# First attention: another order of the query blocks, scores issued further ahead, denominators spread later and copied to SBUF

## The reference

```
q, k, v = _proj_heads(layernorm(x), w_q / w_k / w_v, 16)        # b h s d, d = 16
mask    = triu(-1e8, k=1)
scores  = einsum('bhqd,bhkd->bhqk', q, k) / sqrt(16) + mask
attn    = softmax(scores)
out     = einsum('bhqk,bhkd->bhqd', attn, v)  ->  b s 256  ->  @ w_o
x       = x + out
```

## Time and profile before

| what | us |
|---|---|
| median of 3 runs | 1849.44 |
| lowest and highest run | 1846.48, 1849.45 |
| the profiled execution's own time | 1850.58 |
| its span | 1848.7 |
| TensorE busy in the span | 1626.4 (88%) |
| ScalarE busy in the span | 960.8 (52%) |
| exps of this phase (L711), 640 of them, busy | 514.0 |
| idle time of ScalarE ahead of them | 39.1 |
| weighing matmuls of this phase (L776), busy | 298.9 |

### The profile page before, as it was taken

One profiled execution on the slowest core, in us unless ns is written; L12 is line 12 of the kernel. 1 busy time (PEld: TensorE's weight loads), 2 busy tenths in 40 slices (PEclk: granted clock), 3 DMA queues, 4 the chain that ended last, 5 costly groups with the idle time before them and its releaser, 6 DMA issues. The chain is left out here.

```text
span 1848.7 us, 30826 instructions
## 1 busy us (share of the span) xinstructions
PE 1626.4 (88%) x10249; PEld 1107.8 (60%) x10250; DVE 922.6 (50%) x1792; ACT 960.8 (52%) x1528; POOL 455.8 (25%) x498
## 2 busy tenths in 40 slices
PE   7769999999999966999649999999668977998998
PEld 5632222322222316888638888888567976897887
DVE  6524434434433435777563333333275555755885
ACT  5459999999999953444242222222133335343332
POOL 0001111111111211555542222222153003000674
PEclk9969999999999987999869999999978997998999
DMA  8981415405415019221231111111212010000001
GB/s 265 277 249 35 69 26 93 76 21 91 75 25 88 18 26 326 88 88 46 72 111 48 50 50 51 51 48 51 91 46 92 1 58 0 1 1 4 24 23 46
DMA packets 79455, 134.18 MB, mean 73 GB/s; under 512 B 11600, under 2 KB 45904, under 8 KB 76208
## 3 DMA queue, kind: packets, MB, share of 16 engines
q1 hardware_dynamic: 72360, 111.86, 23.4%
q0 software_dynamic: 6992, 20.95, 3.5%
HBM read 74.63 MB, written 58.14 MB: 72 GB/s over the span
## 5 line engine op out<-in xcount | busy, mean ns | idle before, releaser
L711 ACT ACTIVATE probs<-ps_s 128x1024 f32<-128x1024 f32 (+3 forms) x640 | 514.0, 953 | 39.1 <-PE ps_s L759 36.1
L776 PE MATMUL ps_o<-probs,V 128*17 128x512 f32 (+3 forms) x2560 | 298.9, 539 | 0.3
L699 POOL TENSOR_SCALAR_AFFINE_SELECT probs<-probs 128x512 f32<-128x512 f32 x128 | 86.4, 676 | 468.1 <-ACT probs L711 464.2
L724 DVE COPY weighted<-ps_o 128x512 f32<-128x512 f32 x32 | 22.1, 690 | 255.2 <-PE ps_o L776 255.2
L759 PEld LDWEIGHTS ps_s<-Q_even,K_even 50*128 50x128 f32 x640 | 56.7, 189 | 152.2 <-ACT probs L711 129.4
L1393 DVE COPY slot_hT<-ps_hT 128x512 f32<-128x512 f32 x71 | 49.1, 692 | 194.9 <-PE ps_hT L1436 186.4
L759 PE MATMUL ps_s<-Q_even,K_even 50*128 50x512 f32 (+3 forms) x640 | 128.8, 452 | 18.6 <-DMA Q_even<-shift_parts 10.8
L731 DVE RECIPROCAL inv_denominator<-ps_o 128x512 f32<-128x512 f32 x32 | 107.5, 3358 | 74.5 <-PE ps_o L790 74.5
L759 PEld LDWEIGHTS ps_s<-Q_odd,K_odd 50*128 50x128 f32 x640 | 55.2, 183 | 139.6 <-ACT probs L711 125.6
L1446 PE MATMUL ps_slot_y<-we_out,slot_hT 128*128 x568 | 134.6, 380 | 1.8 <-issue 1.0
L1926 POOL TENSOR_TENSOR h_lo<-h,h_hi 128x512 fp32r<-128x512 f32 x64 | 89.5, 1416 | 181.5 <-DVE h L1972 181.5
(11 more groups left out here) (279 smaller groups left out, 3947.5 us busy)
## 6 DMA issues: line engine op xcount, KB each, us to landing
qk_stacks<-qk_hi SPq DMA_DIRECT2D x64, 256.0 KB, 3.9
slot_rows<-slots_in SPq DMA_DIRECT2D x71, 128.5 KB
qk_stacks<-qk_lo SPq DMA_DIRECT2D x32, 256.0 KB, 4.0
Q_odd<-qk_stacks SPq DMA_DIRECT2D x8, 768.0 KB
K_odd<-qk_stacks SPq DMA_DIRECT2D x8, 768.0 KB
Q_even<-qk_stacks SPq DMA_DIRECT2D x6, 768.0 KB
K_even<-qk_stacks SPq DMA_DIRECT2D x6, 768.0 KB
X<-x SPq DMA_DIRECT2D x8, 512.0 KB, 4.2
```

The costliest lines, as they stand in the source:

```text
L699: pool.affine_select(out=block_of, in_=block_of, compare_op=ALU.is_ge, fill=0.0, base=0, pattern=[[0, HG], [1, P]], channel_multiplier=-1) ...
L711: act.activation(probs[:, at % PROB_BUFS, 2 * p:2 * p + 2, off:BT], ps_s[:, s % SCORE_BUFS, :, off:BT], ACT.Exp).then_inc(exp_ok, 1)
L776: last = pe.matmul(ps_o[32 * h:32 * h + DH + 1, q % 2, off:BT], k["V"][:, group, SEQ_TILES * b + t, h, :], probs[:, at % PROB_BUFS, h, off ...
```

## The change

The order of the blocks within a unit becomes 2, 0, 3, 1 (`TURN`). What used to be counted by `q` (the bank of `ps_o`, the output buffer, the semaphore counts) is counted by the turn `s`, and `q` is looked up only for addresses.

The scores are issued pair by pair. Ahead of the weighing of tile `at`, all pairs below `2 * at + 2 + LEAD` are issued, where LEAD goes by the width of tile `at`: 4 pairs (two tiles ahead) where the tile is 512 or 128 wide, and 6 pairs (three tiles ahead) where it is 384 or 256 wide. In the kernel before it was 4 throughout. The spread of a block's denominators comes after the weighing of the third tile behind the block's last one (the fifth for q = 0), where it was the second. VectorE first copies the spread totals from `ps_o` to SBUF, and then takes the reciprocal within SBUF; the bank of `ps_o` is free from the copy on.

```diff
-    TILE_LIST = [(q, t, max(0, (t - TB * q) * P)) for q in range(SLICES) for t in range(TB * (q + 1))]
+    TURN = (2, 0, 3, 1)
+    TILE_LIST = [(s, t, max(0, (t - TB * TURN[s]) * P)) for s in range(SLICES) for t in range(TB * (TURN[s] + 1))]
...
-    LAG = 2
+    LEAD = {0: 4, P: 6, 2 * P: 6, 3 * P: 4}
+    SPREAD_AFTER = [5 if q == 0 else 3 for q in TURN]
...
                         dve.wait_ge(picked_ok, n + 1)
-                        dve.reciprocal(inv[:, :], ps_o[:, q % 2]).then_inc(norm_ok, 1)
-                        dve.wait_ge(norm_ok, 3 * n + 1)
-                        dve.tensor_tensor(result[:, :], sums[:, q % 2], inv[:, :], ALU.mult).then_inc(norm_ok, 1)
+                        dve.tensor_copy(inv[:, :], ps_o[:, s % 2]).then_inc(norm_ok, 1)
+                        dve.wait_ge(norm_ok, 4 * n + 1)
+                        dve.reciprocal(inv[:, :], inv[:, :]).then_inc(norm_ok, 1)
+                        dve.wait_ge(norm_ok, 4 * n + 2)
+                        dve.tensor_tensor(result[:, :], sums[:, s % 2], inv[:, :], ALU.mult).then_inc(norm_ok, 1)
...
                     if t == 0 and n >= 2:
-                        pe.wait_ge(norm_ok, 3 * (n - 2) + 1)
+                        pe.wait_ge(norm_ok, 4 * (n - 2) + 1)
...
-                for at in range(len(STEPS) + LAG + 2):
-                    if at < len(STEPS):
-                        scores(at)
-                    if 0 <= at - LAG < len(STEPS):
-                        weigh(at - LAG)
-                    if at - LAG - 2 >= 0:
-                        u, g = STEPS[at - LAG - 2]
-                        if g in LAST:
-                            spread_denominators(u, LAST.index(g))
+                scored = 0
+                for at in range(len(STEPS) + SPREAD_AFTER[-1]):
+                    if at < len(STEPS):
+                        for s in range(scored, min(2 * at + 2 + LEAD[TILE_LIST[STEPS[at][1]][2]], 2 * len(STEPS))):
+                            scores(s)
+                            scored = s + 1
+                        weigh(at)
+                    for s in range(SLICES):
+                        u, g = divmod(at - SPREAD_AFTER[s], NT)
+                        if u >= 0 and g == LAST[s]:
+                            spread_denominators(u, s)
```

More of the change, by code:

```diff
@@ L616, in phase_attention @@
     SLICES = SEQ // BT
-    TILE_LIST = [(q, t, max(0, (t - TB * q) * P)) for q in range(SLICES) for t in range(TB * (q + 1))]
+    TURN = (2, 0, 3, 1)
+    TILE_LIST = [(s, t, max(0, (t - TB * TURN[s]) * P)) for s in range(SLICES) for t in range(TB * (TURN[s] + 1))]
     NT = len(TILE_LIST)
-    LAST = [max(g for g, (q, _, _) in enumerate(TILE_LIST) if q == s) for s in range(SLICES)]
-    DIAG = [g for g, (q, t, _) in enumerate(TILE_LIST) if t >= TB * q]
+    LAST = [max(g for g, (at, _, _) in enumerate(TILE_LIST) if at == s) for s in range(SLICES)]
+    DIAG = [g for g, (s, t, _) in enumerate(TILE_LIST) if t >= TB * TURN[s]]
     STEPS = [(u, g) for u in range(UNITS) for g in range(NT)]
     SCORE_BUFS, PROB_BUFS = 3, 4
-    LAG = 2
+    LEAD = {0: 4, P: 6, 2 * P: 6, 3 * P: 4}
+    SPREAD_AFTER = [5 if q == 0 else 3 for q in TURN]
     LOADS = STACK_LOADS + 2
@@ L673, in _ @@
                     g, b = group_and_batch(u)
-                    for q in range(SLICES):
-                        sp.wait_ge(result_ok, SLICES * u + q + 1)
+                    for s, q in enumerate(TURN):
+                        sp.wait_ge(result_ok, SLICES * u + s + 1)
                         for n, out in enumerate((out_hi, out_lo)):
@@ L679, in _ @@
                                 sp.dma_start(io["attended"][n, b, row:row + DH, q * BT:(q + 1) * BT],
-                                             out[32 * h:32 * h + DH, q % 2].bitcast(F32)).then_inc(stored[q % 2], 16)
+                                             out[32 * h:32 * h + DH, s % 2].bitcast(F32)).then_inc(stored[s % 2], 16)
                     if u + 2 < UNITS:
@@ L720, in _ @@
                 for u in range(UNITS):
[L721 to L724, removed]
+                    for s in range(SLICES):
+                        n = SLICES * u + s
+                        dve.wait_ge(pv_ok, NT * u + LAST[s] + 1)
+                        dve.tensor_copy(sums[:, s % 2], ps_o[:, s % 2]).then_inc(sums_ok, 1)
@@ L725, in _ @@
                         dve.wait_ge(sums_ok, 3 * n + 1)
-                        dve.tensor_copy(sums_hi[:, :], sums[:, q % 2]).then_inc(sums_ok, 1)
+                        dve.tensor_copy(sums_hi[:, :], sums[:, s % 2]).then_inc(sums_ok, 1)
                         dve.wait_ge(sums_ok, 3 * n + 2)
-                        dve.tensor_tensor(sums_lo[:, :], sums[:, q % 2], sums_hi[:, :].bitcast(F32), ALU.subtract
+                        dve.tensor_tensor(sums_lo[:, :], sums[:, s % 2], sums_hi[:, :].bitcast(F32), ALU.subtract
@@ L738, in _ @@
-                        dve.wait_ge(norm_ok, 3 * n + 3)
-                        dve.tensor_tensor(out_lo[:, q % 2], result[:, :], out_hi[:, q % 2].bitcast(F32), ALU.subtract
+                            dve.wait_ge(stored[s % 2], 16 * ROWS_OUT * (n // 2))
+                        dve.tensor_copy(out_hi[:, s % 2], result[:, :]).then_inc(norm_ok, 1)
+                        dve.wait_ge(norm_ok, 4 * n + 4)
+                        dve.tensor_tensor(out_lo[:, s % 2], result[:, :], out_hi[:, s % 2].bitcast(F32), ALU.subtract
@@ L744, in _, with scores @@
                 pe.wait_ge(zero_ok, 1)
-                def scores(at):
+                def scores(s):
+                    at, p = s // 2, s % 2
                     u, g = STEPS[at]
                     j = u % 2
-                    q, t, off = TILE_LIST[g]
-                    if g == 0:
+                    turn, t, off = TILE_LIST[g]
+                    q = TURN[turn]
+                    if g == 0 and p == 0:
                         pe.wait_ge(loaded[j], 16 * LOADS * (u // 2 + 1))
@@ L753, in scores @@
                             pe.wait_ge(ones_in, 32)
[L754 to L763, removed]
+                    if s >= SCORE_BUFS:
+                        pe.wait_ge(exp_ok, s - SCORE_BUFS + 1)
+                    for h in range(2):
+                        last = pe.matmul(ps_s[:, s % SCORE_BUFS, h, off:BT],
+                                         K[j][HALF * h:HALF * h + USED_ROWS, p, t * P:(t + 1) * P],
+                                         Q[j][HALF * h:HALF * h + USED_ROWS, p, q * BT + off:(q + 1) * BT],
+                                         start=True, stop=True)
+                    last.then_inc(scores_ok, 1)
                 def weigh(at):
                     u, g = STEPS[at]
-                    q, t, off = TILE_LIST[g]
+                    s, t, off = TILE_LIST[g]
                     group, b = group_and_batch(u)
-                    n = SLICES * u + q
+                    n = SLICES * u + s
                     if t == 0 and n >= 2:
-                        pe.wait_ge(norm_ok, 3 * (n - 2) + 1)
+                        pe.wait_ge(norm_ok, 4 * (n - 2) + 1)
                     pe.wait_ge(exp_ok, 2 * at + 2)
@@ L775, in weigh, with spread_denominators @@
                     for h in range(HG):
-                        last = pe.matmul(ps_o[32 * h:32 * h + DH + 1, q % 2, off:BT],
+                        last = pe.matmul(ps_o[32 * h:32 * h + DH + 1, s % 2, off:BT],
                                          k["V"][:, group, SEQ_TILES * b + t, h, :],
                                          probs[:, at % PROB_BUFS, h, off:BT],
-                                         start=(t == 0), stop=(g == LAST[q]))
+                                         start=(t == 0), stop=(g == LAST[s]))
                     last.then_inc(pv_ok, 1)
-                def spread_denominators(u, q):
-                    n = SLICES * u + q
+                def spread_denominators(u, s):
+                    n = SLICES * u + s
                     if n == 0:
@@ L788, in spread_denominators @@
                     rows = pick[:, :, :].rearrange("p h r -> p (h r)")
-                    pe.matmul(ps_o[:, q % 2], rows, sums_hi[:, :], start=True, stop=False)
-                    pe.matmul(ps_o[:, q % 2], rows, sums_lo[:, :], start=False, stop=True).then_inc(picked_ok, 1)
-                for at in range(len(STEPS) + LAG + 2):
+                    pe.matmul(ps_o[:, s % 2], rows, sums_hi[:, :], start=True, stop=False)
+                    pe.matmul(ps_o[:, s % 2], rows, sums_lo[:, :], start=False, stop=True).then_inc(picked_ok, 1)
+                scored = 0
+                for at in range(len(STEPS) + SPREAD_AFTER[-1]):
                     if at < len(STEPS):
-                        scores(at)
-                    if 0 <= at - LAG < len(STEPS):
-                        weigh(at - LAG)
-                    if at - LAG - 2 >= 0:
-                        u, g = STEPS[at - LAG - 2]
-                        if g in LAST:
-                            spread_denominators(u, LAST.index(g))
```

(8 more changed lines are left out.)

4 lines of the change are left out of this document (1 added, 3 removed).

## The result

The changed kernel took 1825.12 us in the median of 4 runs (1815.60 to 1826.54) against 1848.63 us, the median before once a fourth run is added to the three above; the ratio is 0.9864, with a 95% interval of 0.9829 to 0.9898. Measured once more later, on one chip with three variants, it took 1819.28 us against 1844.82, ratio 0.9853 (0.9829 to 0.9877). So the two differences of medians are 23.5 and 25.5 us. Its profiled execution took 1826.54 us, with a span of 1824.7 us.

What follows compares the result with a forecast made beforehand. ScalarE was taken as the bound wherever the order lets TensorE be ahead. Seven units' 25.9 us plus the first's 1.5, less 0.7 for the copy, give 26.7 us off 1850.58: 1823.9, stated as 1823, range 1813 to 1839.

Steps and rivals of the forecast that it cites:

- TensorE's 60.6 us: TensorE's work in one unit of the first attention, summed from step times: 2.5 us less than ScalarE's.
- a loop that no order takes out: At each block change: exp frees bank, scores, signals, exp tail, 0.75 us against two short exps' 0.56; 0.19 us gap stays.
- restarts: ScalarE starting late after a gap: about 0.1 us each, four in a unit; fewer late ones gain about 0.4 us.
- The price of 1.8 us: Gain a unit from issuing the next block's first scores before the 384-wide weighing: 0.46 us at each of four block changes.
- the spreads' 1.4: Gain a unit from moving the denominator spreads later: 0.75 + 0.46 + 0.2 us of ScalarE's gaps.
- the unit laid out against ScalarE's floor: One attention unit: ScalarE's 63.1 us floor, plus four 0.19 us gaps, four 0.1 us gaps and four 0.1 us restarts, 64.7 us.
- TensorE's stand of 2.4 us: Without the copy, TensorE would wait 2.4 us at q = 3's first weighing for its bank.
- 15.4 us at 2.99 us a tile: First unit's half-clock start: 5.1 full tiles losing 1.16 us each, 6 us, less 1 us for first pairs ahead: 5.
- +0.7 us for the copy: In the phase's last block the added VectorE copy lies on the path, costing 0.7 us once.
- first rival: The three score buffers bound TensorE anyway, so the lead does nothing; only the spreads' gain is left: 1840 us, chance 0.10.
- The masks are not held up: Rival said the SBUF reciprocal delays GpSimd's mask at q = 1's first diagonal tile: 16 us over eight units, 1839, chance 0.05.
- The slower case: Rival: at block changes the later 384-wide weighing holds the exp of the tile four on; 1868 us, chance 0.05.

## Why the prediction was right, and where only by luck

The forecast was 1823 us, 26.7 us less than before in the profiled execution; measured were 24.0 us there, and 23.5 and 25.5 us in the two medians. The unit was forecast rightly; that the total fits is partly luck. The phase itself got 29.3 us shorter in that profile: 4.1 us of gain in the first unit were not in the forecast, 1.5 us of loss at the end neither. The rest of the kernel then took 5.6 us more in this run, and hid the difference.

- **The bound.** Two engines near full, ScalarE the busier, and the order the question: right. The unit came to 64.62 us for a forecast of 64.7. TensorE's 60.6 us no run measures by itself.
- **What is left in a unit.** I had 0.19 us at each block change, by a loop that no order takes out. That step was wrong: no gap over 0.05 us is left at any block change. Ahead of one 128-wide tile there are 0.27 us, where I had 0.1. The sum fits since two errors cancel: the gaps over 0.05 us sum to 0.7 us in a unit, where I had 1.16, and the exps keep ScalarE busy for 511.9 us in eight units, 64.0 a unit, where I had 63.1 and 0.4 for restarts.

```profile
L713 ACT ACTIVATE probs<-ps_s 128x1024 f32<-128x1024 f32 (+3 forms) x640 | 511.9, 941 | 9.9 <-PE ps_s L763 6.4
```

- **The lead.** The mechanism was right, as TensorE's rows show. The price of 1.8 us was wrong as a price of a part: alone it brings 1.3 us, and taking it away from the whole costs 2.9.
- **The sum of parts.** This step failed as a way of working. I added the lead's 1.8, the spreads' 1.4 and the restarts' 0.4 as if each had its own gain. Taken away singly from the whole, the lead costs 2.9 us a unit, the copy 3.7, the distance of the spreads 4.5 to 5.5, the order 0.5: together over three times the gain of 3.8. The distance of the spreads can eat more than all of it by itself, the copy nearly all, the lead three quarters. What held was the other sum, the unit laid out against ScalarE's floor.
- **The copy.** TensorE's stand of 2.4 us without it was right to 0.1 us. That the bank would be free 0.2 us before it is wanted was not: the first weighing of q = 3 waits 0.36 us for the copy (2.9 us in 8 times), and TensorE can afford it. The reciprocal from SBUF takes 3.35 us, as from PSUM. I gave the stand no price by the clock: the slow restart costs 1.16 us beside the 2.22 that ScalarE waits for the stand.
- **The order.** I counted nothing. It is 0.46 us a unit, 3 us over seven.
- **The first unit.** I forecast 69.7 us and it took 65.57. The step "15.4 us at 2.99 us a tile" took the length of the half clock from the kernel before. In this kernel it ended 8 us sooner. That is 4.1 us of gain that the forecast did not have.
- **The end of the phase.** I had +0.7 us for the copy; it was +2.2. The copy is 0.7 of it; the rest is that VectorE was still busy with q = 3 when q = 1's last tile was weighed, and began 645.87 instead of about 644.8, and that the last spread ran at the lower clock (matmuls of 0.80 and 0.63 us for 0.50 and 0.39).

```profile
643.70 1.07 DVE L737 TENSOR_TENSOR attention_result<-weighted,inv_denominator 128x512 f32<-128x512 f32 x1
...
645.87 0.68 DVE L726 COPY weighted<-ps_o 128x512 f32<-128x512 f32 x1
...
647.79 0.80 PE L793 MATMUL ps_o<-weighted_hi,denominator_pick 128*128 128x512 f32 x1 [3.01 <-DVE weighted_lo L730]
648.38 0.63 PE L794 MATMUL ps_o<-weighted_lo,denominator_pick 128*128 128x512 f32 x1
```

- **Rivals.** The lead does something (first rival refuted by the kernel without it). The masks are not held up by a reciprocal that reads SBUF: of the 128 masks 32 lie beside one, and none of these takes over 0.64 us. The longest of all, beside `weighted_lo`, is 0.82 us, shorter than the 1.19 of the earlier trace rows. That agrees with the first half of the rule of the Trainium skill ("SBUF — State Buffer", Who interferes with whom): one SBUF input outside the two-port modes does not contend.

```profile
L701 POOL TENSOR_SCALAR_AFFINE_SELECT probs<-probs x128: 629/634/818, 142.8 to 643.6; 128x512 f32<-128x512 f32 x128
```

- **The slower case.** The mechanism that I gave (a weighing that holds ScalarE's exp of the tile four on) showed in no kernel: no row has ScalarE released by L780. What can make such a change slower, the runs show twice: with the spreads two behind TensorE waits for VectorE and its clock falls (ratio 1.0067), and with lead 6 throughout a weighing stands ahead of each block's first scores (1.0020).

## What to carry to other kernels

Where two engines are both within a few per cent of their floor, lay out one whole period against the busier one's floor, and don't add up what single edits remove: the edits here take out obstacles in series, and without the copy, or with the spreads where they were, all the others together are worth next to nothing or less. A fixed lookahead does not help at a place where the work per step shrinks on one engine and not on the other; a lookahead that grows just there, by one step, does. For a stand of TensorE like those of 2.44 and 2.95 us here, reckon with a slow restart beside the stand: it followed 15 of 16 of them.

## What the runs showed of the hardware

- As TensorE's stand of 2.44 us ended, the granted clock fell to the lower level in seven of eight units, and stayed at 1.00 in one; with a stand of 2.95 us it fell in all eight. The slow restart cost ScalarE 1.16 us. Stands of 1.34 and 1.01 us a unit (the lead alone) left it at 1.00, as did waits of 0.36 us.
- At the phase's start the clock rose 7 to 10 us after the first exp in the ten profiles with full 512-wide tiles first, and 10 to 15 us after it in the three with the narrow tiles of q = 0 first. Of the latest of the ten (lead 6 throughout) and the earliest of the three (the lead alone) the times are 9.8 and 10.4 us, so the two groups nearly touch.
- A reciprocal over 128 x 512 in fp32 takes 3.35 us from SBUF and 3.36 from PSUM.
- In the new schedule other instructions of VectorE with two SBUF operands meet the masks: `weighted_lo` took 769 ns in the mean instead of 693, and 1.00 us where it lay beside a mask; `attention_result` 1.07 us there instead of 0.69. `attention_lo`, which met them before (up to 1.17 us), took 0.69 throughout.
